# Products with a stationary operand of zeros ahead of the gathered rows in the edge pass of a graph network kernel

## What is computed

```
src, dst = edge_index[0], edge_index[1]
msg_input = concatenate([x[src], x[dst], edge_attr], axis=-1)
h = relu(msg_input @ W1.T + b1)
messages = h @ W2.T + b2
agg = segment_sum(messages, dst, num_segments=n)
upd = relu(agg @ Wu.T + bu)
y = x + upd
return layernorm(y) * gamma + beta
```

## Time and profile before

| | us |
|---|---|
| median of 3 runs | 2182.67 |
| lowest and highest | 2176.24, 2184.08 |
| the profiled execution | 2173.5 |
| its span | 2171.7 |
| TensorE busy | 1444.7 |
| VectorE busy | 1010.8 |
| GpSimd busy | 838.6 |
| ScalarE busy | 660.5 |

### The profile page before, as it was taken

The page is one execution under the profiler, slowest core; times in us unless marked ns, Lnnn a source line. Parts: engine busy times, 40 slices in busy tenths (PEclk is TensorE's granted clock), DMA queues, the critical chain, the costliest instruction groups (busy, mean ns, idle before and its releaser), DMA issues. The chain is left out here.

```text
span 2171.7 us, 31085 instructions
## 1 busy us (share of the span) xinstructions
PE 1444.7 (67%) x10698; PEld 951.5 (44%) x10698; DVE 1010.8 (47%) x2912; ACT 660.5 (30%) x1704; POOL 838.6 (39%) x877
## 2 busy tenths in 40 slices
PE   3235455555555555544555555699899999899997
PEld 3123334343343333433334343356666666455544
DVE  7745556555555555555556555431442224311101
ACT  2213344333433343333334333111343333100000
POOL 5636666666666666655666664000000000000001
PEclk8656665665555665666656666799999999899998
DMA  6543444434434444433344443103110001871770
GB/s 194 145 90 110 117 125 117 120 112 125 124 112 118 129 118 113 113 111 111 111 128 117 118 116 108 30 12 139 33 29 1 10 6 40 302 265 69 263 293 29
DMA packets 200850, 245.75 MB, mean 113 GB/s; under 512 B 36794, under 2 KB 174053, under 8 KB 200674
## 3 DMA queue, kind: packets, MB, share of 16 engines
q1 hardware_dynamic: 171202, 177.71, 25.6%
q0 software_dynamic: 29472, 65.73, 11.3%
HBM read 174.00 MB, written 55.93 MB: 106 GB/s over the span
## 5 line engine op out<-in xcount | busy, mean ns | idle before, releaser
L983 POOL DMA_INDIRECT arena<-dram_PHL,src_of x786 | 760.3, 967 | 472.5 <-remote 215.0
L1287 PE MATMUL psum<-arena 128*128 128x100 f16 x1568 | 225.9, 251 | 265.2 <-issue 179.7
L1287 PEld LDWEIGHTS psum<-arena 128*128 128x128 f16 x1568 | 179.6, 131 | 398.7 <-issue 372.5
L1271 PE MATMUL psum<-arena 128*128 128x128 f16 x1612 | 191.4, 284 | 165.7 <-issue 94.6
L1197 ACT ACTIVATE arena<-psum 128x512 f16<-128x512 f32 x202 | 120.4, 596 | 592.3 <-remote 439.5
L1289 PE MATMUL psum<-arena 128*128 128x50 f16 x1568 | 216.4, 232 | 77.2 <-issue 76.7
L1271 PEld LDWEIGHTS psum<-arena 128*128 128x128 f16 x1612 | 144.6, 129 | 188.0 <-issue 184.9
L1040 DVE SCALAR_TENSOR_TENSOR agg_all<-psum,agg_all 128x64 f32<-128x64 f32 x202 | 44.5, 220 | 379.3 <-remote 371.4
L1289 PEld LDWEIGHTS psum<-arena 128*128 128x128 f16 x1568 | 175.9, 116 | 88.3 <-issue 86.2
L1276 PE MATMUL psum<-arena 128*128 128x512 f16 x404 | 188.0, 554 | 14.0 <-issue 13.6
L2436 PE MATMUL psum<-arena,parts_b 128*128 128x512 fp8e4 (+5 forms) x875 | 171.0, 354 | 3.2 <-PEq L2858 3.2
(11 more groups left out here) (345 smaller groups left out, 2126.9 us busy)
## 6 DMA issues: line engine op xcount, KB each, us to landing
dram_aw<-aw_out SPq DMA_DIRECT2D x196, 200.0 KB
arena<-dram_aw SPq DMA_DIRECT2D x6, 6400.0 KB, 20.2
arena<-dram_aw SPq DMA_DIRECT2D x3, 4800.0 KB
arena<-in_ea_quads SPq DMA_DIRECT2D x51, 256.0 KB
arena<-dram_rel SPq DMA_DIRECT2D x51, 256.0 KB
arena<-arena SPq DMA_DIRECT2D x408, 32.0 KB
arena<-dram_PHL,src_of POOLq DMA_INDIRECT x806
arena<-dram_aw SPq DMA_DIRECT2D x2, 4000.0 KB, 13.3
```

The lines of the kernel that those rows point to most:

```text
L983: nc.gpsimd.indirect_dma_start(gathered_p[:, slot, k, :], None, d["PHL"], bass.IndirectOffsetOnAxis(ap=src_of[:, b:b + 1], axis=0)).then_i ...
L1271: nc.tensor.matmul(out[:, k * P:(k + 1) * P], side[:, s, at:at + P], node_side[:, g % NAB, part * D:(part + 1) * D], start=(part == 0 and ...
L1287: nc.tensor.matmul(out, hot_lo[:, u, p, :], hot_key[:, u, p, 0:2].rearrange("p a k -> p (a k)"), start=True, stop=False)
```

## The change

A tile `still` of 128x128 half-precision zeros is added and cleared once by VectorE. In `build(g)`, between the eight products of L1271 and the wait for the gathered rows, TensorE runs STILL = 8 products of 128x512 with this tile as the stationary operand, and the same tile repeated four times as the moving one. They accumulate into the bank of the step, so they add zeros. The first step waits once until the tile is cleared.

```diff
+        still = sb("still", [P, P], F16)
...
+        STILL = 8
...
+        still_made = new("still_made")
...
+                nc.vector.memset(still[:, :], 0.0).then_inc(still_made, 1)
                 nc.vector.memset(last[:, :], 0.0).then_inc(cleared, 1)
...
+                    if g == 0:
+                        pe.wait_ge(still_made, 1)
+                    for _ in range(STILL):
+                        nc.tensor.matmul(out.rearrange("p (a e) -> p a e", e=P), still[:, :],
+                                         still[:, :].rearrange("p (a e) -> p a e", a=1).broadcast_to([P, n, P]),
+                                         start=False, stop=False)
                     pe.wait_ge(gathered[g % NPG], 16 * sum(blocks_of(k) for k in range(g % NPG, g + 1, NPG)))
```

## The result

The changed kernel takes 2211.43 us (median of 4 runs, 2208.64 to 2212.79) beside 2183.38 us of the kernel before (2176.24 to 2184.84): a ratio of 1.0137, 95% interval 1.0121 to 1.0153. It is slower by 28 us.

A forecast was written before the change was run, and what follows sets the result against it. GpSimd's gather ring was taken to pace the edge pass at 6.05 us a step. Terms 65 - 10 + 0.5, about +55 us on 2173.5, gave 2229, about 2235 against the median; forecast's range 2200 to 2275, overall 2080 to 2320.

The forecast's parts named there:

- The wait for gathered rows gives no cover: Before L1276 in the edge pass: TensorE's wait is already over, 14.0 us idle in the whole program.
- The price of the products: Eight new products a step on TensorE: 1.7 us at the high clock, 3.4 at the low, 2.6 taken.
- The clock rises: Sign: TensorE's granted clock in the edge pass goes from 0.62 to 0.80 to 0.95.
- The rival built on it: Higher clock wins: products keep TensorE from standing in the edge pass, time falls to 2083 us; chance 0.26.
- TensorE busy over 80%: Sign: TensorE's busy share in the edge pass would exceed 80%.
- GpSimd's idle time for TensorE goes from 269 to over 320 us: Sign: GpSimd waits longer for TensorE before its gathers; a fall would favour the higher-clock rival.
- The relu's remote wait stays near 440 or grows: Sign: ScalarE's relu wait for a remote release stays near 440 us or grows by L1276's lateness.
- the ring's: Gather slot loop: L1276's end frees GpSimd's slot and starts the relu; later products delay it, 65 us.
- half of the 101 pairs: Pairs of edge-pass steps: 50 assumed to start GpSimd's fifth gather 1.3 us late, 65 us.
- a credit of 10: L1271, L1276 and L1301 run faster at a higher clock: 0.1 us over 100 steps, 10 us back.
- All is hidden: Rival: GpSimd's gathers set the 6.05 us step and TensorE's idle time covers the products; 2183 us, chance 0.17.
- The clock stays low: Rival: the clock doesn't follow the zero products in the edge pass, steps take 6.6 us; 2290 us, chance 0.12.

The follow-up runs named there:

- e2: The changed kernel with sixteen products of zeros a step in place of eight: 2217.9 us, ratio 1.0227 to the kernel before.
- e10: The changed kernel, unaltered, run again beside the kernel before at the lower level: 1991.35 us, ratio 1.0209.
- e6: The kernel before with two of four gathers a step from the fifth step on, plus the eight products: 1977.09 us, ratio to before 1.0138.
- e11: The kernel before with two of four gathers a step from the fifth step on, at the lower level: 1924.38 us, ratio 0.9876.
- e3: The changed kernel with its eight products moved behind the row products, to the start of `multiply`: 2190.54 us, ratio 1.0111 to before.
- e9: The kernel before, unchanged, run again for its profile at the lower level: 1955.49 us in its one run.
- e12: The changed kernel with six store buffers in place of three, half of the weights copied and stored twice: 2189.75 us, ratio 1.0096 to before.
- e4: The kernel before with two of four gathers a step from the fifth step on, beside before at the upper level: 1943.68 us, ratio 0.896.

## Why the prediction was right, and where not

The forecast was 2235 us, slower; measured were 2211.43. By its steps:

- *The wait for gathered rows gives no cover.* Right for the profile it was read from: 14.0 us before, 0.0 after. It isn't a property of the kernel, though: at the lower level that wait is 145.9 us, and the kernel loses there too (1.0209).
- *The price of the products*, 1.7 us at the high and 3.4 us at the low clock, 2.6 taken. Measured: 1.89 and 2.98 us in two steps, 2.35 us in the mean. This agrees, and so does the 0.21 us between two at the high clock: e2's sixteen take 3.62 us, 0.22 from one start to the next if the last lasts 0.38. That stream of products at a clock of 0.99 does not come near the 131 ns of the Trainium skill (TensorE: Matmul & The Clock Gate, section Back-to-back issue gap).
- *The clock rises*, to 0.80 to 0.95: 0.88. The rule of the Trainium skill (TensorE: Matmul & The Clock Gate, section Why this matters for your kernels), that long pauses cost the clock, agrees with 0.62, 0.72, 0.88 and 0.99 with none, two, eight and sixteen products. The rival built on it fell, since the time rose with eight and again with sixteen. *TensorE busy over 80%* was wrong: 71% (707.76 of 1000 us), because the older products took less time at the higher clock: the row products 129.1 us in place of 188.0.
- *GpSimd's idle time for TensorE goes from 269 to over 320 us*: 332.5 (255.1 + 77.4). *The relu's remote wait stays near 440 or grows*: 619.8.
- *The term that was mis-sized is the ring's*: "half of the 101 pairs pay 1.3 us each because the products lie ahead of L1276", +65 us with a credit of 10. The time rose by 28 us (39 between the profiled executions). The half of the pairs was chosen without a count, and GpSimd's stops give one: 69 steps began without a stop, so there were about 69 such pairs and not 50, which by the same price makes 90 us. The price failed more than the count, in two ways. The place is at most a part of it: behind the row products they cost 1.0111. And pairs don't get longer, they disappear: 196 stops in place of 128, each shorter (332.5/196 = 1.70 us in place of 269.1/128 = 2.10 us). In the pass as a whole, pauses that were there and the time that the faster clock gives back take in most of the 2.35 us; the rest is 39.3/202 = 0.19 us a step. So the direction came from a reading that holds (the row products are late for GpSimd), and the size fell into the range partly by luck, with a count too low and a price too high.
- *Two slips in the sums* change nothing: 202 x 0.5 us are 101 us and not 110, and 2182.67 + 55 is 2238, where 2235 was forecast.
- *TensorE's idle time before L1287 and L1271 was left unexplained*: 179.7 of the 265.2 us and 94.6 of the 165.7 us are called issue, that is, no wait is found. At the lower level they are nearly absent, as the last section shows.
- *All is hidden* fails beyond two products (1.0005 with two at the upper level, 1.0048 with four at the lower). *The clock stays low* fails with 0.88.

What is shown: the loss doesn't need the late results (e10), nor the gathers as the pace (e6 with e11), and most of it doesn't need the place ahead of the row products (e3); a clock of 0.99 doesn't make up for it (e2). At the lower level it arises where TensorE had little wait for rows to give (e9 with e10). What stays open is how the upper level turns the products into one stop in every step, since what delays TensorE and its results there isn't known, and how much the waits for a store buffer add at the lower level; e12 was made for that and met the other level.

## What to carry to other kernels

A wait that a profile shows is a place for free work only where it lies; look at its count, its longest and above all its place in time beside its total before filling it (145.9 us here were 65 waits of up to 4.8 us in 202 steps, most of them before the stretch in which the loss arose). Products that only raise TensorE's clock have to win more on the bounding loop than they take: here the way from 0.62 to 0.99 came with a time longer by 2.3%. Take a new profile of the kernel before whenever its time differs from that of the first one, since this kernel has two levels with different waits.

## What the runs showed of the hardware

The same kernel takes 2168.56 to 2183.38 us in some groups of runs and 1948.96 or 1949.47 us in others, and both levels were met within one group. At the upper level 106 of the 202 relus end with a wait called remote, 439.5 us in all, and the two stretches of the earlier trace rows show such results taken 1.6 to 2.1 us after GpSimd's last gather in a row. It isn't so in every step: the relu at 316.83 us in the earlier trace rows starts 1.17 us after its products, in the middle of eight gathers. In e9's profile at the lower level no wait is remote, the gathers take 968 ns as at the upper one (967), and the clock of the stretch 300 to 1300 us is 0.75 in place of 0.62.

TensorE itself is late too at the upper level. It stands before its products where the profile finds no wait (us in total, times, longest; first the kernel before at the upper level, then e9's one line of this kind above 1 us for these products):

```profile
PE psum L1287 <- issue: 179.7, 137, 9.4
PE psum L1271 <- issue: 94.6, 105, 2.5
PE psum L1289 <- issue: 76.7, 86, 2.4
```

```profile
PE psum L1271 <- issue: 3.5, 9, 1.0
```

In the earlier trace rows this falls into the same place as the late results: while GpSimd's gathers run to 310.96 us, the products of `multiply` start one by one,

```profile
309.86 0.20 PE L1289 MATMUL psum<-arena 128*128 128x50 f16 x1 [1.42 <-issue]
...
311.35 0.20 PE L1289 MATMUL psum<-arena 128*128 128x50 f16 x1 [1.20 <-issue]
```

and from 312.77 us on they follow each other closely. Two gathers a step in place of four bring the time to 1943.68 us (e4) beside before at the upper level, near what the same kernel takes beside before at the lower one (1924.38 in e11). What decides the level, and what holds TensorE and its results back, no run here tells.
